# Causal attention: joined remainders, five score banks in two sizes, and a head output that lies in one bank and is read by VectorE alone

## What is computed

```python
q = heads(x @ Wq + bq); k = heads(x @ Wk + bk); v = heads(x @ Wv + bv)
scores = jnp.einsum('bhqd,bhkd->bhqk', q, k) * (1.0 / np.sqrt(hd)) + bias[None]   # -1e9 beyond the diagonal
attn = jax.nn.softmax(scores, axis=-1)
out = jnp.einsum('bhqk,bhkd->bhqd', attn, v)
```

## Time and profile before

| | us |
|---|---|
| median of three runs | 3126.15 (3125.51 to 3127.25) |
| the profiled execution | 3123.28 |
| its span, first to last instruction | 3121.1 |
| outside the span | 2.2 |
| mean granted TensorE clock | 0.935 of full speed |
| busy, 420 to 994 us (574 us): TensorE | 480.2 |
| VectorE | 427.6 |
| ScalarE | 434.5 |
| GpSimd | 572.1 |

### The profile page before, as it was taken

One profiled execution on the slowest core, in us unless ns is written; L12 is line 12 of the kernel. 1 busy time (PEld: TensorE's weight loads), 2 busy tenths in 40 slices (PEclk: granted clock), 3 DMA queues, 4 the chain that ended last, 5 costly groups with the idle time before them and its releaser, 6 DMA issues. The chain is left out here.

```text
span 3121.1 us, 77095 instructions
## 1 busy us (share of the span) xinstructions
PE 2634.2 (84%) x24119; PEld 1431.1 (46%) x24119; DVE 2318.2 (74%) x4525; ACT 1762.4 (56%) x3255; POOL 1874.1 (60%) x1424
## 2 busy tenths in 40 slices
PE   7999478888886869999999999980999899703999
PEld 3555235555554534555555555550444344301444
DVE  8888667777775767888888888867333467697776
ACT  3444257777775435666666666654233477696333
POOL 3444479999997317999999999996100144300000
PEclk9999779999998988999999999995999999856999
DMA  8999724444445662222122131115644588797332
GB/s 305 336 334 342 267 96 134 136 126 131 135 133 169 235 202 60 53 75 66 51 80 62 49 98 50 47 54 172 214 153 158 200 278 281 258 415 282 110 126 81
DMA packets 320920, 511.28 MB, mean 164 GB/s; under 512 B 35669, under 2 KB 155221, under 8 KB 320810
## 3 DMA queue, kind: packets, MB, share of 16 engines
q1 hardware_dynamic: 317674, 503.65, 48.3%
q0 software_dynamic: 1952, 6.29, 0.6%
q10 hardware_dynamic: 1184, 0.01, 0.0%
HBM read 270.95 MB, written 194.28 MB: 149 GB/s over the span
## 5 line engine op out<-in xcount | busy, mean ns | idle before, releaser
L1102 POOL TENSOR_TENSOR cross_plo<-cross_p 128x1024 f16<-128x1024 f32 x448 | 906.6, 2058 | 73.4 <-ACT cross_p L940 69.7
L940 ACT ACTIVATE cross_p<-cross_st 128x512 f32<-128x512 f32 x1024 | 556.2, 595 | 289.1 <-PE cross_st L874 289.0
L1015 DVE CUSTOM_DVE_ANT_0 cross_junk<-cross_sc,rows 128x1024 bf16<-128x1024 f32 x512 | 619.0, 1219 | 110.5 <-PE cross_sc L835 98.2
L1102 POOL TENSOR_TENSOR self_plo<-self_p 128x1024 f16<-128x1024 f32 (+7 forms) x512 | 577.0, 1165 | 19.1 <-ACT self_p L940 18.8
L940 ACT ACTIVATE self_p<-self_st,self_strip 128x512 f32<-128x512 f32 (+3 forms) x768 | 415.3, 582 | 148.0 <-PE self_st L872 116.8
L1015 DVE CUSTOM_DVE_ANT_0 self_junk<-self_sc,self_strip 128x1024 bf16<-128x1024 f32 (+7 forms) x512 | 371.1, 752 | 140.8 <-PE self_sc L835 136.0
L869 PE MATMUL cross_st<-cross_qa,cross_ka 97*128 97x512 f16 x1024 | 390.4, 381 | 2.5 <-ACT cross_p L940 1.7
L874 PE MATMUL cross_st<-rows,idbig 128*128 128x512 f16 x1024 | 389.9, 381 | 0.0
L835 PE MATMUL cross_sc<-cross_ka,cross_qa 96*128 96x512 f16 x1024 | 311.3, 386 | 22.3 <-DMA cross_ka<-scr_k_hi 16.7
L897 PEld LDWEIGHTS cross_o<-cross_vh,cross_p 128*128 128x128 bf16 x4096 | 270.1, 97 | 75.0 <-issue 21.7
L897 PE MATMUL cross_o<-cross_vh,cross_p 128*128 128x65 f16 x4096 | 297.4, 191 | 4.6 <-POOL cross_plo L1102 4.2
(11 more groups left out here) (254 smaller groups left out, 5710.3 us busy)
## 6 DMA issues: line engine op xcount, KB each, us to landing
self_strip<-self_strips SPq DMA_DIRECT2D x68, 516.0 KB, 3.2
scr_gate<-gt_y SPq DMA_DIRECT2D x96, 256.0 KB, 2.1
v_w<-scr_gate SPq DMA_DIRECT2D x96, 256.0 KB, 4.1
scr_h<-v_w SPq DMA_DIRECT2D x96, 256.0 KB, 4.0
j_h<-scr_h SPq DMA_DIRECT2D x48, 512.0 KB, 9.6
d_o<-scr_o SPq DMA_DIRECT2D x9, 1536.0 KB
scr_up<-v_y SPq DMA_DIRECT2D x48, 256.0 KB, 4.3
j_u<-scr_up SPq DMA_DIRECT2D x24, 512.0 KB, 12.0
```

The source lines that it names most:

```text
L940: nc.scalar.activation(p32[u % NPR][:, q0:q1], stp[cc % 2][:, 0:q1 - q0], ACT.Exp, bias=bias, scale=SM).then_inc(expd, 1)
L1015: nc.vector.tensor_tensor_reduce(junk[slot % 2][:, 0:w], sc[slot % 2][:, 0:w], bias, 1.0, -3e38, ALU.add, ALU.max, qmax[n % 2][:, qt:qt + ...
L1102: nc.gpsimd.tensor_tensor(plo[u % NPR][:, q], p32[u % NPR][:, q], high[:, q], ALU.subtract).then_inc(lo_g, 1)
```

## The change

In the causal stage alone:

- **Score tiles.** Three instead of two: two of 1024 columns for the wide tiles, which take turns, and one of 512 columns for all the narrow ones. TensorE may write a wide tile when the maxima of the tile four before are done, a narrow one as before when those of the tile two before are.
- **Remainders.** `p32` and `plo` become eight buffers of 1152 columns, and a wide tile and the narrow one behind it lie in one, side by side. GpSimd computes the remainder of both with one instruction over 1152 columns, when the second is there: 4 instructions a head instead of 8.
- **Head output.** One bank instead of two, 33 columns for each 128 queries. The values need three matmuls instead of two for every 128 queries: high half by 33 columns, high half by the 32 low value columns into the same place, remainder by 33 columns.
- **How a head ends.** ScalarE copies nothing. VectorE waits for the head's last matmul, takes the reciprocal straight from the bank and multiplies straight from the bank into `ost` (`finish`, two instructions in place of `gather`'s and `scale`'s four). This stands in VectorE's list where `gather` stood, and the next head's first values wait for the multiply.
- **Leads.** `SLEAD` 21 instead of 19, `ELEAD` 8 instead of 6. Cross attention keeps its numbers of tiles, leads and instructions.

```diff
+        SLEAD, ELEAD, NPP = (21, 8, 8) if causal else (19, 6, 4)
+        NPR = PAIR * NPP
+        PW = S + P if causal else PAIR * S
...
-        sc = [kit.ps(f"{name}_sc{j}", [P, S]) for j in range(2)]
+        sc = [kit.ps(f"{name}_sc{j}", [P, GT if j == 2 else S]) for j in range(3 if causal else 2)]
...
-        ob = [kit.ps(f"{name}_o{j}", [P, ST // 2, VW]) for j in range(2)]
+        ob = [kit.ps(f"{name}_o{j}", [P, ST, HD + 1] if causal else [P, ST // 2, VW]) for j in range(1 if causal else 2)]
...
+        def score_bank(u):
+            if not causal:
+                return sc[u % 2]
+            return sc[2] if u % PAIR else sc[u // PAIR % 2]
+        def score_distance(u):
+            return 2 * PAIR if causal and u % PAIR == 0 else 2
...
+        def lows_of(u):
+            j, b = spot(u)
+            if on_vector(u) or causal and u % PAIR == 0 and not on_vector(u + 1):
+                return None
+            if causal and u % PAIR == 1 and not on_vector(u - 1):
+                return j, 0, b + width(u)
+            return j, b, b + width(u)
...
-                    pe.wait_ge(taken, i * (HB * UH) + slot + 1)
+                    freed = slot + 3 - score_distance(u)
+                    if not isinstance(i, int) or i * (HB * UH) + freed > 0:
+                        pe.wait_ge(taken, i * (HB * UH) + freed)
...
-                        pe.wait_ge(o_read, (i * HB + n) * 2 + 2)
+                        if causal:
+                            pe.wait_ge(o_scaled, i * HB + n + 1)
+                        else:
+                            pe.wait_ge(o_read, (i * HB + n) * 2 + 2)
...
+                        if causal:
+                            nc.tensor.matmul(out[:, row, :], high[:, q], vh[n % NQK][:, kt, 0:HD + 1], start=first, stop=False, skip_group_check=True)
+                            nc.tensor.matmul(out[:, row, 0:HD], high[:, q], vh[n % NQK][:, kt, HD + 1:VW], start=False, stop=False, skip_group_check=True)
+                        else:
+                            nc.tensor.matmul(out[:, row, :], high[:, q], vh[n % NQK][:, kt, :], start=first, stop=False, skip_group_check=True)
+                        mm = nc.tensor.matmul(out[:, row, 0:HD + 1], rest[:, q], vh[n % NQK][:, kt, 0:HD + 1],
...
-                    if t % UH == UH - 1:
+                    if not causal and t % UH == UH - 1:
                         n = t // UH
...
+                def finish(i, n):
+                    head = i * HB + n
+                    dve.wait_ge(pv_done, i * (HB * UH) + (n + 1) * UH + PRIME)
+                    dve.wait_ge(o_scaled, head + 1)
+                    nc.vector.reciprocal(rden[n % 2][:], ob[0][:, :, HD]).then_inc(o_recip, 1)
+                    dve.wait_ge(o_recip, head + 1)
+                    if n % HB == 0:
+                        dve.wait_ge(o_out, i * 16)
+                    nc.vector.tensor_tensor(ost[:, :, n % HB * HD:(n % HB + 1) * HD], ob[0][:, :, 0:HD],
+                                            rden[n % 2][:].unsqueeze(2).to_broadcast([P, ST, HD]), ALU.mult).then_inc(o_scaled, 1)
...
                     n = to_finish(i, t, 0)
                     if n is not None:
-                        gather(i, n)
+                        (finish if causal else gather)(i, n)
                     ahead(i, t + SLEAD, last)
```

75 lines of the change are left out of this document (43 added, 32 removed).

## The result

| | before | after |
|---|---|---|
| median of the runs, us | 3126.41 (3125.51 to 3127.25) | 3202.76 (3162.15 to 3223.55) |
| ratio to before, 95% interval | | 1.0167, 1.013 to 1.0203 |
| the profiled execution, us | 3123.28 | 3195.9 |
| its span, us | 3121.1 | 3193.8 |
| first values matmul of the self stage | 420.4 | 419.0 |

The forecast was 3127.5 with a range to 3144. The kernel is slower by more than that, and unevenly: its four runs lie 61 us apart, where those of before lie 2 us apart. The ratio's interval leaves out the highest runs; by the medians it is 1.024.

The account below looks back on a forecast made before the run. GpSimd (9.0 us a head) and a TensorE-VectorE ring (9.03) both bound the self stage. 0.10 us more for 61 heads, less 4.7 at the start, gave +1.4: 3127.5 us, range 3105 to 3144, the forecast's own 3115 to 3140.

Parts of the forecast that it names:

- Nothing changes in cross attention: Cross attention, after the self stage: no change in time, so no term for it.
- the sum: Whole kernel: 0.10 us a head over 61 heads less 4.7 at the start, +1.4 us, giving 3127.5 on the median.
- rival 4: GpSimd's 1152-column instruction is dear: at 2878 ns each, a head takes 11.5 us, 3274 in all; chance 0.03.
- GpSimd, and that it is worth nothing alone: Self stage: joined remainders take GpSimd 8.27 us a head, 0.76 less, worth nothing unless the TensorE-VectorE chain falls too.
- The guess on the 1024 columns: GpSimd's excess at 1024 columns comes from something beside it, perhaps VectorE's 0.70 us multiply with both inputs in SBUF.
- The third matmul: Values on TensorE: 36 triples a head at 0.079 us a matmul add 0.86 us a head; 0.62 before the 768-wide scores.
- the way from first values to the scores of place 4: TensorE, from a head's first values to its 768-wide tile's scores: 6.58 us, against 6.56 to the 896-wide tile's before.
- End of a head: VectorE's reciprocal 0.31 to the next start and multiply from the bank 0.42: together 0.73 us where 0.48 stood.
- The ring of this kind of head: Closed chain TensorE, maxima, end of head, TensorE in the self stage: 8.96 us a head, against 8.89 before.
- Score banks: Third score tile removes TensorE's waits for maxima two tiles before a wide tile: 0 to 0.3 us a head.
- The edges: Self stage start: key scores begin some 4.7 us earlier; the larger lead is paid at the start, given back at the end.
- Rival 1, the ring does not close: TensorE's first values matmul is ready later than VectorE finishes, so 8.3 us a head counts: 49 less, 3077; chance 0.13.

Follow-up runs that it names:

- experiments 1 to 3: Idle TensorE instructions ahead of the cross loop: changed kernel with 158, 3133.05 us, 40, 3118.31, 16, 3182.85; kernel before with 98, 3231.1, 158, 3140.53, 82, 3129.72.
- experiments 3 and 4: 3: changed kernel, 40 idle instructions at self stage head, 3118.73 us; 4: kernel before, 70 per cross round, 3302.0 and 3296.38, 90, 3333.23 and 3335.38, 110, 3385.6 to 3428.14.
- experiment 6: Changed kernel, well placed: single remainders 3115.1 us; end of head ahead of 768-wide maxima 3092.12; both 3106.58; the second with idle instructions at program start 3091.79.
- experiment 5: Kernel before with joined remainders alone: 3182.02 us; changed kernel, well placed, without third score tile: 3132.21; that with leads 19 and 6: 3161.07.
- place 176: Cross loop starting 176 behind a multiple of 256: changed kernel as it is, 3202.76 us; kernel before with 98 idle TensorE instructions ahead of it, 3231.1 us.
- 192: Changed kernel with 16 idle TensorE instructions ahead of cross attention, so its loop starts 192 behind a multiple of 256: 3182.85 us.

## Why the prediction was wrong

**The step that failed** is "Nothing changes in cross attention", and with it the sum, which had no term for it. The change leaves that code as it is, but moves it: 80.4 us in the profiled execution, against a sum of +1.4. That the place does it is shown by moving the loop in both kernels (experiments 1 to 3); that what counts is how many blocks of 256 it touches is well supported (experiments 3 and 4). Nothing in the profile of before told that a place can be bad. But the number of instructions that the change adds ahead of a loop with no gap was there to be counted, and so were the instruction packets, 52 in all and none in the attention loops after their first round. No rival had it. The figure that came nearest to the time, 3182 us by what the Trainium skill (GPSIMD Engine Reference, section 3.1) says of a GpSimd element, came near by accident: 1152 columns take 2.11 us and not 2.5. Two slips in the working change nothing: by its own line the eight widths sum to 9.30 us, not 9.32, and rival 4 to 3273, not 3274.

**The rest, with the loop in its place**, is 3118.3 to 3118.7 us, inside the forecast's own range of 3115 to 3140, on the fast side:

- *GpSimd, and that it is worth nothing alone*: 8.43 us a head and 37.9 us idle, as forecast but for 0.04 us an instruction; single remainders cost nothing (experiment 6). The guess on the 1024 columns fits too: with joined remainders alone the GpSimd instruction in which the multiply ends takes 2.29 us where its neighbours take 2.11, and where the multiply reads a bank all take 2.11.
- *The third matmul*: the way from first values to the scores of place 4 took 6.50, forecast 6.58. As forecast it went into waits for ScalarE: from 430 to 960 us TensorE's matmuls of key scores (L869, now L909) waited 39.5 us for exponentials before and 22.1 after.
- *End of a head*: reciprocal to multiply 0.23 (forecast 0.31), multiply 0.42 (0.42), and 0.14 to the next values (0.06). The ring of this kind of head is 8.88, forecast 8.96; a mean head 9.00, forecast 9.13, so 61 heads are 8 us better than the sum.
- *Score banks*: 0.09 us a head, inside the bound of 0 to 0.3; at the start 6.9 us, forecast 4.7. Of this the stage kept only 1.4 at its first values (420.4 to 419.0), since the larger leads are paid for there (4.9 us, experiment 5).
- *The edges*: forecast 4.7 us less. The stage ends 5.5 us earlier in all: 1.4 at the first values, 1.4 in the two heads before the last (7.68 and 7.63 us, before 8.38 and 8.30), 1.4 in the last head's own values (3.8 us, before 5.2), and some 1.2 in the 61 heads before these.
- *The leads*, to which I gave no worth in the steady heads: right only in passing. Without them, with two score tiles, a head takes 0.72 us more, 44 us in 61 heads (experiment 5). The forecast walked through the steps with the new leads and never asked what the old ones would do.
- *Rival 1, the ring does not close*: the ring did close, so it was rightly refused. But half of its 49 us could be had: one place's shift of `finish` took 26 us out and left a head at 8.58, close above GpSimd's 8.43.

## What to carry to other kernels

When a change alters how many instructions an engine has ahead of a loop, look at every later loop of that engine: note its length and how many blocks of 256 it touches (here blocks begin at 203 of the count, not at 0), and look for instruction packets inside its rounds in both traces. A stretch that got slower with the same instructions, waits put down to "issue" at the loop's head and runs that scatter are the signs, and a few idle instructions ahead of the loop, where the engine waits anyhow, are test and cure. And of two engines that are both full, take the ring apart first: an order in one list (reciprocal ahead of 768-wide maxima) was worth 26 us, the cheaper GpSimd instruction nothing before it and 14 to 18 us after.

## What the runs showed of the hardware

- A TensorE loop of 1569 instructions ran with no more than one packet in all its rounds from eight of the starts tried, and with nine of 16 KB a round from two. A fetched round costs 8 us at place 176 and 9 at 192; in the one looked at, 5.3 are gaps and the rest is the clock at the lower level behind them.
- The second stop of a fetched round comes at the same instruction of the count, 203 behind a multiple of 256, whether the loop starts at 176 or at 192: there a block begins. The two bad starts are among the 32 from which a loop of 1569 instructions then touches eight blocks, the eight good ones are not.
- At a bad place whether a round fetches is not fixed: at place 176 ten in a row did and then three did not, or in one run none; at 192 every second one. Why is open.
- VectorE's multiply with both inputs in SBUF ends 0.28 us behind the GpSimd instruction beside it, in 59 heads of 59 and 54 of 54: 0.70 us in the mean beside ones of 1.04 us, 1.55 beside ones of 2.11. The same size read from a bank takes 0.42 always (423 to 426 ns). The Trainium skill (GPSIMD Engine Reference, section 1, Specifications) has the two engines' SBUF interface shared, with contention for VectorE instructions with two SBUF inputs. The trace agrees.
- An idle semaphore increment on TensorE costs between nothing (40 at the start), some 0.1 us (158 ahead of cross attention, 15 us) and 0.18 us (70 in the full loop).
